# Reordering the splits of x1, x2 and x3 in the last stage of a four-layer residual chain on one core

## The reference

```python
x = x + L0(x)   # gated MLP, 512 -> 1376 -> 512, with one of 16 low-rank adapters per batch
x = x + L1(x)   # einsum('bct,bcd->bdt', x, weights[condition]): a 32x32 mix of the channels of a batch
x = x + L2(x)   # below
x = x + L3(x)   # a second 32x32 channel mix, chosen by the same condition
# L2:
base = jnp.einsum('btd,od->bto', x, W)
logits = jnp.einsum('btd,ed->bte', x, Wr) + bias              # 8 experts
topw, topi = jax.lax.top_k(logits, 2)
gates = jnp.sum(jax.nn.one_hot(topi, E) * jax.nn.softmax(topw, axis=-1)[..., None], axis=-2)
h = jnp.einsum('btd,erd->bter', x, A)
out = base + 2.0 * jnp.einsum('bter,bte,eor->bto', h, gates, B)
```

## Time and profile before

| | us |
|---|---|
| median of 3 runs | 572.92 (571.8 to 574.95) |
| the profiled execution's own time | 574.08 |
| its span, first to last instruction | 572.3 |
| busy in the span: TensorE matmuls | 550.4 (96%) |
| VectorE | 313.9 (55%) |
| ScalarE | 208.2 (36%) |
| GpSimd | 207.8 (36%) |
| start of pass 1, of pass 2, of pass 15 | 465.81, 473.54, 560.25 |
| mean granted clock | 0.997 |

### The profile page before, as it was taken

One profiled execution on the slowest core, in us unless ns is written; L12 is line 12 of the kernel. 1 busy time (PEld: TensorE's weight loads), 2 busy tenths in 40 slices (PEclk: granted clock), 3 DMA queues, 4 the chain that ended last, 5 costly groups with the idle time before them and its releaser, 6 DMA issues.

```text
span 572.3 us, 8728 instructions
## 1 busy us (share of the span) xinstructions
PE 550.4 (96%) x3172; PEld 494.1 (86%) x3172; DVE 313.9 (55%) x718; ACT 208.2 (36%) x415; POOL 207.8 (36%) x236
## 2 busy tenths in 40 slices
PE   6899999999999999999999999999999998889897
PEld 6789988898989898989898989898898988778785
DVE  6697354545464454554545454545444666566665
ACT  6584232433334243332323323232323433433332
POOL 5642144756566665614141413232212221221100
PEclk9999999999999999999999999999999998999999
DMA  8983356575766665746465545565548323565531
GB/s 285 365 264 138 111 158 195 172 218 163 228 208 186 211 208 181 237 154 202 146 187 163 175 160 167 185 177 163 172 166 287 120 82 130 198 198 185 167 129 74
DMA packets 72027, 104.68 MB, mean 183 GB/s; under 512 B 9392, under 2 KB 39728, under 8 KB 71984
## 3 DMA queue, kind: packets, MB, share of 16 engines
q1 hardware_dynamic: 60960, 66.82, 35.7%
q0 software_dynamic: 10880, 37.23, 21.2%
q10 hardware_dynamic: 144, 0.06, 0.0%
HBM read 77.87 MB, written 26.21 MB: 182 GB/s over the span
## 4 chain that ended last, share of the span: by engine, by line
PE 89%; issue 4%; DMA 3%; ACT 1%; DVE 1%; SPq 1%; POOL 0%; ACTq 0%; DVEq 0%
PE gu_ps L1351 13%; PE gu_ps L1353 13%; PE gu_ps L1352 13%; PE down_ps L1351 8%; PE down_ps L1352 8%; PE down_ps L1353 8%; PE l_ps L1351 6%; PE l_ps L1353 5%; PE l_ps L1352 5%; PE gu_ps L1358 3%; PE gu_ps L1359 3%; DMA bd<-bd_hl 1%; DMA act_blocks<-act 1%; PE down_ps L1358 1%; PE down_ps L1359 1%
## 5 line engine op out<-in xcount | busy, mean ns | idle before, releaser
L1351 PE MATMUL down_ps<-wd_sb,act_hl 128*128 128x288 f32 (+1 forms) x352 | 105.1, 299 | 0.6 <-DVE act_hl L1108 0.4
L1352 PE MATMUL down_ps<-wd_sb,act_hl 128*128 128x288 f32 (+1 forms) x352 | 103.8, 295 | 0.0
L1353 PE MATMUL down_ps<-wd_sb,act_hl 128*128 128x288 f32 (+1 forms) x352 | 103.6, 294 | 0.0
L792 POOL DMA_INDIRECT b_sel_raw<-b_gu,idx_rank x48 | 46.4, 968 | 156.6 <-PE gu_ps L1359 145.7
L1351 PE MATMUL gu_ps<-w_sb,xt 128*128 128x512 f32 x256 | 102.0, 398 | 0.0
L1353 PE MATMUL gu_ps<-w_sb,xt 128*128 128x512 f32 x256 | 100.4, 392 | 0.0
L1352 PE MATMUL gu_ps<-w_sb,xt 128*128 128x512 f32 x256 | 100.3, 392 | 0.0
L792 POOL DMA_INDIRECT a_raw<-a_all,idx_batch x60 | 66.4, 1107 | 60.7 <-DVE wd_sb L1108 46.7
L1172 DVE TENSOR_TENSOR act<-act,gu_ps 128x512 f32<-128x512 f32 (+1 forms) x47 | 29.8, 634 | 98.0 <-ACT act L915 73.5
L915 ACT ACTIVATE act<-gu_ps 128x512 f32<-128x512 f32 (+1 forms) x47 | 26.1, 555 | 147.0 <-PE gu_ps L1359 147.0
L1351 PEld LDWEIGHTS down_ps<-wd_sb,act_hl 128*128 128x128 f32 (+1 forms) x352 | 66.1, 188 | 2.8 <-DVE act_hl L1108 0.8
(11 more groups left out here) (159 smaller groups left out, 1055.3 us busy)
## 6 DMA issues: line engine op xcount, KB each, us to landing
act_blocks<-act SPq DMA_DIRECT2D x39, 256.0 KB
x_res<-act_blocks SPq DMA_DIRECT2D x156, 64.0 KB
xt_raw<-x_t SPq DMA_DIRECT2D x16, 256.0 KB
w_sb_raw<-wgu SPq DMA_DIRECT2D x16, 256.0 KB
x_res<-x_rows SPq DMA_DIRECT2D x16, 256.0 KB
x_after_l<-x_res SPq DMA_DIRECT2D x16, 256.0 KB
bd<-bd_hl SPq DMA_DIRECT2D x16, 256.0 KB
x<-x_after_l SPq DMA_DIRECT2D x16, 256.0 KB, 2.8
```

Of the source, the lines that this page charges most:

```text
L792: nc.gpsimd.indirect_dma_start(out=dst, out_offset=None, in_=table, in_offset=bass.IndirectOffsetOnAxis(ap=idx, axis=0)).then_inc(s, 16)
L1351: pe.matmul(out_, stationary[0], moving[0], start=start, stop=False, skip_group_check=True)
L1352: pe.matmul(out_, stationary[0], moving[1], start=False, stop=False, skip_group_check=True)
L1353: return pe.matmul(out_, stationary[1], moving[0], start=False, stop=stop, skip_group_check=True)
```

## The change

On ScalarE, inside the loop, x2 is split ahead of the exponential, and x1 (with its wait for a DMA) goes behind x3 and behind the copy of y. One `high_x1(3)` and one `high_x2t(15)` outside the loop move in the same way. On VectorE, `low_x3` goes ahead of `route_weights`. The x3 of tile 13 is copied by ScalarE and no longer by VectorE, with a semaphore of its own (`s_x3`, while VectorE's copies now count on `s_x3b`), and the copy of x3 of tile 14 goes behind `low_hgt(15)`. No other instruction is added or removed, no DMA is moved and TensorE's order is the same.

```diff
@@ -409,7 +409,8 @@
 
         def x3_count(t, n=0):
 
-            return t - PLAIN + n + 1
+
+            return (s_x3, 1) if t == PLAIN else (s_x3b, t - PLAIN + n)
 
         def base_of(t, a, b):
 
@@ -488,6 +489,7 @@
         s_hgtlo = sem("s_hgtlo")
         s_l2 = sem("s_l2")
         s_x3 = sem("s_x3")
+        s_x3b = sem("s_x3b")
         s_x3hi = sem("s_x3hi")
         s_x3lo = sem("s_x3lo")
         s_l3 = sem("s_l3")
@@ -984,6 +986,10 @@
                 sc.wait_ge(s_l2, t + 1)
                 sc.copy(halves(x3_hl[:, t % 2, 0, :], 0, H), base_of(t, 0, H)).then_inc(s_x3hi, 1)
 
+            def copy_x3(t):
+                sc.wait_ge(s_l2, t + 1)
+                sc.copy(halves(x3[:, t % 3, :], 0, H), base_of(t, 0, H)).then_inc(s_x3, 1)
+
             def copy_y(t, n=0):
                 if 2 <= t < NT - 1:
                     sc.wait_ge(s_out[t % 2], 16 * (t // 2))
@@ -1032,10 +1038,10 @@
                         high_x1(2)
                         high_w2(HC)
                         exponential(0)
+                        high_x1(3)
                     job_hi(job)
                     if job == ("td", NT - 1):
                         high_x2t(1)
-                        high_x1(3)
                 if 0 <= s - W13_FIRST - 1 < NT:
                     high_bd(s - W13_FIRST - 1)
                 if s == STEPS - 2:
@@ -1045,17 +1051,17 @@
             for i in range(NT - 2):
                 if i >= 1:
                     high_hgt(i - 1)
+                    high_x2t(i + 1)
                     exponential(i)
-                    high_x2t(i + 1)
-                if i + 4 < NT:
-                    high_x1(i + 4)
-                if i >= 1:
                     high_x3(i - 1)
                 if i >= 2:
                     copy_y(i - 2)
+                if i + 4 < NT:
+                    high_x1(i + 4)
             high_hgt(NT - 3)
+            high_x2t(NT - 1)
             exponential(NT - 2)
-            high_x2t(NT - 1)
+            copy_x3(NT - 3)
             exponential(NT - 1)
             high_hgt(NT - 2)
             copy_y(NT - 4)
@@ -1273,7 +1279,7 @@
             def copy_x3(t):
                 for n, (a, b) in enumerate(pieces(t)):
                     ve.wait_ge(s_l2, t + n + 1)
-                    ve.tensor_copy(halves(x3[:, t % 3, :], a, b), base_of(t, a, b)).then_inc(s_x3, 1)
+                    ve.tensor_copy(halves(x3[:, t % 3, :], a, b), base_of(t, a, b)).then_inc(s_x3b, 1)
 
             def copy_y(t, n):
                 a, b = pieces(t)[n]
@@ -1323,23 +1329,22 @@
                 low_hgt(i - 1)
                 route_top(i)
                 low_x2t(i + 1)
+                low_x3(i - 1)
                 route_weights(i)
-                low_x3(i - 1)
                 route_gates(i)
                 if i + 3 < NT:
                     take_x2(i + 3)
             low_hgt(NT - 3)
             route_top(NT - 2)
             low_x2t(NT - 1)
-            copy_x3(NT - 3)
             route_weights(NT - 2)
             route_gates(NT - 2)
             route_top(NT - 1)
             low_hgt(NT - 2)
             route_weights(NT - 1)
             route_gates(NT - 1)
+            low_hgt(NT - 1)
             copy_x3(NT - 2)
-            low_hgt(NT - 1)
             copy_x3(NT - 1)
             copy_y(NT - 1, 1)
 
@@ -1487,7 +1492,7 @@
                     if t == 1:
                         pe.wait_ge(s_x1, NT)
                     if t >= 2:
-                        pe.wait_ge(*((s_x3lo, t - 1) if t - 2 < PLAIN else (s_x3, x3_count(t - 2))))
+                        pe.wait_ge(*((s_x3lo, t - 1) if t - 2 < PLAIN else x3_count(t - 2)))
                         pe.wait_ge(s_hg, t - 1)
                 for c in range(c0, c1):
                     if t == 0 and half == 1:
@@ -1527,7 +1532,7 @@
                     mix(l3_of(t, 0), t, 1, x3_hl).then_inc(s_l3, 1)
                     return
                 for n, (a, b) in enumerate(pieces(t)):
-                    pe.wait_ge(s_x3, x3_count(t, n))
+                    pe.wait_ge(*x3_count(t, n))
                     pe.matmul(l3_of(t, n), bd13_hl[:, t % BD, 0, 1, :].bitcast(F32), x3[:, t % 3, a:b],
                               start=True, stop=True, skip_group_check=True).then_inc(s_l3, 1)
 
```

## The result

The changed kernel takes 558.51 us in the median (558.17 to 561.52, four runs), against 573.62 (571.8 to 574.95, four runs) for the kernel before: a ratio of 0.975, 95% interval 0.9706 to 0.9795. (The ratios here come from all the runs and not from the two medians, whose quotient is 0.974.) The profiled execution took 558.51 with a span of 556.7.

What follows compares the result with a forecast made beforehand. TensorE, 96% busy, bounds the kernel; only its waits and low clock can be won. Waits 10.3 + restarts 2.0 - leftovers 0.24 + first matmuls 0.9 + clock 1.48 + start 0.13 = 14.6 us, giving 558.8; 8-in-10 range 556.0 to 563.5.

Steps and rivals of the forecast that it cites:

- two cases: Median forecast: 558.3 if the median gains all 14.6 us, 559.8 if it has no low-clock stretch and gains 13.1.
- What ended last: Ahead of most passes: x3 lay ready 1.5 us while ScalarE waited for x1's DMA; twelve TensorE waits, 10.3 us.
- The times after T: Forecast starts of instructions in the changed loop, counted from T, a pass's first TensorE matmul; next pass at T+5.92.
- The low clock: Behind the wait ahead of pass 2: one stretch took 4.35 us instead of 2.87; 1.48 won if it goes too.
- Pass 2: The pass holding the low-clock stretch: 1.48 us forecast to be won there.
- The start: First passes: earlier x1(3) removes a TensorE wait, 0.4 with restart; td mask perhaps 0.3 late; net 0.13 us.
- The GpSimd rival: Chance 0.04: GpSimd's low x1 holds VectorE's L1255 if low x3 is over 0.4 late; 7.5 us in 11 passes, 566.
- x2's landing: Chance 0.05: x2 loads land 1 us later, delaying low x2t and low x3; 0.4 in each of 11 passes, 563.

Runs made afterwards that it cites:

- s1_x1_last: Kernel before with only ScalarE's loop edited, high x1 moved behind x3 and the copy of y: 562.87 us, ratio 0.983.
- a1_x1_ahead: Changed kernel with x1 put back ahead of x3 in ScalarE's loop, all else as changed: 572.94 us, ratio 1.001 to the kernel before.
- a2_copy13_vector: Changed kernel with x3 of tile 13 copied by VectorE again, behind low x2t(15): 560.27 us, ratio 0.977 to the kernel before.
- a5: Changed kernel with x1 behind x3 but ahead of the copy of y in ScalarE's loop: 560.85 us, ratio 0.978 to the kernel before.
- a7_exp_first: Changed kernel with the exponential ahead of x2t again in ScalarE's loop: 565.58 us, ratio 0.978 to the kernel before.
- v1_x3_first: Kernel before with VectorE's part of the loop alone, low x3 ahead of route_weights: 574.98 us, ratio 1.003.
- after_again: The changed kernel itself, unaltered, run once more in a later session: 564.02 us, ratio 0.975 to the kernel before.

## Why the prediction was right

- **The forecast** of 558.8 was met by 558.51, and for the profiled execution 15.6 came instead of 14.6. That the numbers met this closely is in part luck: 0.87 of the 15.6 lies before pass 0, where the executions of one kernel differ by more than that, and 558.8 was a value taken between two cases.
- **What ended last** was x3 behind x1 on ScalarE, as predicted. Shown: s1_x1_last moves this alone and wins 1.7% of the 2.5%; a1_x1_ahead takes this alone back and loses all.
- **The times after T** held to 0.1: x2t 2.27 (forecast 2.35), x3 3.82 (3.85), low x3 4.44 (4.53), L1261 6.14 (6.24), x1 5.88 (5.92), GpSimd 6.59 (6.62). Passes 3 to 13 won 10.03, forecast 9.95; pass 14 0.98, forecast 0.94.
- **The low clock** was the step that failed: "1.48, if it goes with the wait". One stretch in one profile was put in the sum, with the wait ahead of it as its cause. The waits of 1.56, 2.12 and 2.34 at full clock show that such a wait does not suffice. Nor does the stretch belong to the median. At 0.62 over 4.35 us it takes 0.003 off the mean granted clock of an execution, and of the 17 executions of the kernel before in the first session of experiments nine have a mean of 1.000, the median one (572.78) among them. The nine have a median of 571.87, the seven at 0.997 one of 573.32: 1.45 apart, about the 1.48 of the stretch. Where the clock was low in those seven is not recorded, and a low mean can also come from the start (a1_x1_ahead: 0.996, with 0.97 in the first 60 us). The prediction had put its value between the two cases, and that hid the error.
- **Pass 2** won 1.12: the 1.48 of that stretch, plus 0.26 of small wait and restart that the sum had left out, less 0.62 by GpSimd. The tail without the stretch is 14.7 - 1.5 = 13.2 shorter, against 13.1 forecast without the clock. This agreement hides three misses that cancel: 0.36 more in pass 0, 0.26 more and 0.62 less in pass 2.
- **The start** was taken too low: 0.49 instead of 0.13, outside its own bounds of -0.4 and 0.4. Low x1(3) did hold the operation ahead of the td mask (0.87), but TensorE's transposition of td was not late by it: it starts 0.87 after the transpositions of x2 (L1478, in the changed kernel L1483) in both kernels.
- **The GpSimd rival** is real. It was foreseen for pass 1 ("up to 0.7", measured 0.62), and with it the point from which it decides, low x3 over 0.4 late: in a2_copy13_vector 0.52 late (0.43 behind the forecast T+4.53) held L1260, in the changed kernel 0.36 late (T+4.80 in pass 8) held nothing. In the profile of the changed kernel it delayed TensorE once, in those of a2, a5 and a7 two or three times. It would have been better to put the 0.6 of pass 1 in the sum.
- **What I didn't see** is that the wait for x1 closed a loop through VectorE, the DMA queue and back to ScalarE, and that the length of this loop, not TensorE's work, set the pass. The forecast came right all the same, since the change opens the loop. It is also why VectorE's part, a gain in the changed kernel, is a loss by itself.
- **x2's landing** did get slower, as that rival said it might: the longest landing from 490 on took 3.9 after issue, against the 3.0 of the earlier trace rows that the prediction had used as its bound. ScalarE waited for it in three passes, at most 1.0, and none of that reached TensorE: passes 4, 8 and 11 last 5.84 to 5.85. The room held here, but in a2_copy13_vector and a7_exp_first the same lateness with GpSimd cost 0.7 a time.

## What to carry to other kernels

In a software pipeline with in-order engines, follow a wait around: if the transfer waited for is issued behind work that itself follows the waiting instruction, the pass cannot be shorter than that loop, and an instruction moved into the loop can lengthen each pass, as route_weights did. A wait for a DMA whose data is wanted late belongs behind what the bottleneck engine wants next. And try the parts of an order change apart as well as together: here one part wins 1.7%, another loses 0.3%, and the whole wins 2.5%.

## What the runs showed of the hardware

- **A GpSimd subtraction between SBUF tensors holds some of VectorE's operations and lets others pass.** In the 14 profiles, from 440 us on, take the VectorE operations that began while such a subtraction had 0.4 us or more to go. Held were all with two inputs in SBUF and all 7 `tensor_scalar` over eight elements per partition. Those with two inputs were 39 over one element and 3 over eight, and with the `tensor_scalar` they lasted 0.85 to 1.28 instead of 0.16 to 0.29 and ended 0.01 to 0.03 after GpSimd. Two more, over 648 elements, lasted 1.92 instead of 0.82. Not held were those with an input in PSUM (33 low x3 at 0.69 and 31 take_x2 at 0.70 to 0.72 among them), 21 reciprocals and 21 `tensor_scalar` over one element. So size does not decide. In v1_x3_first, GpSimd's subtraction below has 0.83 to go when the low x3 of 515.52, shown above, starts, and that lasts its usual 0.69.

```profile
515.08 1.27 POOL L856 TENSOR_TENSOR x_hl<-x,x_hl 128x512 fp32r<-128x512 f32 x1 [5.94 <-ACT x_hl L1015]
```

SBUF — State Buffer of the Trainium skill, section SBUF: two separate sides, calls the shared port pair an exclusive lock held for a whole instruction; the 49 small operations that ended 0.01 to 0.03 after GpSimd agree with that. The same page of the Trainium skill, section Who interferes with whom, names `tensor_scalar` among the kinds that can take the pair under conditions; here those over eight elements were held (L1259, 1.21) and those over one were not (0.14).
- **The clock of TensorE** is not a function of one wait: an idle time of 2.04 was followed by a stretch at a granted clock of 0.62, a mix of 1.2 and 2.4 GHz; those of 1.56, 2.12 and 2.34 were followed by full clock, in one profile each.
- **The first 60 us differ between executions.** In the third session the kernels took 5 us more, and the profiles put most of it there. The changed kernel's first 60 us in its first profile and in that of after_again (columns of the earlier trace rows): 296 matmuls against 258, granted clock 1.00 against 0.94. The clock is not all of it: a7_exp_first, in the same session, has 276 at 1.00. Why the start differs is open. The tails of the changed kernel in the two profiles agree within 0.2.

```profile
0.00:60.00 60.00, 53.80 (x296) 47.56 (x297) 45.13 (x86) 37.71 (x71) 31.01 (x30) 1.00 0.78 262
```

```profile
0.00:60.00 60.00, 49.58 (x258) 44.31 (x259) 41.34 (x79) 34.61 (x65) 27.14 (x28) 0.94 0.75 251
```
